# Graph layer on one core: the output projection of one node block per turn of the edge loop instead of a stage of its own

## The reference

```python
h = jnp.maximum(_layernorm(x, axis=-1), 0.0)
eq = h @ Wq + bq
ek = h @ Wk + bk
e = efeat @ We + be
m = jax.nn.relu(eq[dst] + ek[src] + e)
ft = jax.ops.segment_sum(m, dst, num_segments=n_nodes)
return x + (ft @ Wr + br)
```

## Time and profile before

| | us |
| --- | --- |
| median of 3 runs | 1247.06 (1246.17 to 1247.19) |
| the profiled execution | 1248.51 |
| its span | 1246.6 |
| TensorE matmul busy | 1119.9 (90%) |
| VectorE busy | 962.8 (77%) |
| ScalarE busy | 857.2 (69%) |
| GpSimd busy | 887.7 (71%) |

### The profile page before, as it was taken

How to read it: one execution, slowest core, us unless ns; L and a number is a source line. 1 busy time by engine, 2 the same in 40 slices (tenths; PEclk the granted TensorE clock), 3 DMA queues, 4 the chain that set the end, 5 groups by cost and what they waited for, 6 DMA issues and landing times.

```text
span 1246.6 us, 33342 instructions
## 1 busy us (share of the span) xinstructions
PE 1119.9 (90%) x8632; PEld 1051.0 (84%) x8632; DVE 962.8 (77%) x1324; ACT 857.2 (69%) x1463; POOL 887.7 (71%) x946
## 2 busy tenths in 40 slices
PE   1997799999999999999999999999999999999876
PEld 1775789889898888898898988888988989898875
DVE  5887577777777777777777777777777777777798
ACT  1676577777777777777777777777777777777542
POOL 4454777777777777777777777777777777777644
PEclk9999999999999999999999999999999999999989
DMA  8888777777778777777777777777877787877664
GB/s 249 273 275 273 237 244 246 245 244 243 254 246 248 245 246 247 250 248 244 244 245 251 244 252 245 244 247 247 251 246 245 245 248 242 256 244 244 209 191 140
DMA packets 164469, 303.48 MB, mean 243 GB/s; under 512 B 29204, under 2 KB 110740, under 8 KB 164452
## 3 DMA queue, kind: packets, MB, share of 16 engines
q1 hardware_dynamic: 124516, 194.18, 50.0%
q0 software_dynamic: 39936, 109.11, 27.0%
HBM read 275.69 MB, written 27.48 MB: 243 GB/s over the span
## 4 chain that ended last, share of the span: by engine, by line
POOL 46%; issue 37%; PE 9%; DVE 3%; DMA 3%; ACT 1%; POOLq 1%; SPq 0%; DVEq 0%; ACTq 0%
POOL k_rows L494 46%; PE p_sum L934 5%; PE p_edge L934 3%; DVE hT_lo L896 1%; DMA ft<-in_x 1%; PE p_turn L943 1%; DMA k_rows<-k_table,idx 1%; POOLq L502 0%; DMA pre<-in_dst_groups 0%; DMA range_table<-top_g 0%; DVE k_rows L908 0%; DVE k_rows L717 0%; POOLq L492 0%; DVE p_edge L838 0%; ACT hT_hi L655 0%
## 5 line engine op out<-in xcount | busy, mean ns | idle before, releaser
L494 POOL DMA_INDIRECT k_rows<-k_table,idx x832 | 799.3, 961 | 255.9 <-issue 255.0
L934 PE MATMUL p_edge<-we_hi,edge_hi 128*128 128x256 f32 x1664 | 487.0, 293 | 75.9 <-DVE m_lo L846 67.1
L934 PE MATMUL p_edge<-we_lo,edge_hi 128*128 128x256 f32 x1664 | 465.4, 280 | 0.0
L934 PE MATMUL p_edge<-we_hi,edge_lo 128*128 128x256 f32 x1664 | 465.1, 280 | 0.0
L838 DVE TENSOR_TENSOR p_edge<-p_edge,k_rows 128x1024 f32<-128x1024 f32 x208 | 256.4, 1233 | 244.7 <-DMA k_rows<-k_table,idx 244.6
L934 PEld LDWEIGHTS p_edge<-we_hi,edge_hi 128*128 128x128 f32 x1664 | 314.4, 189 | 122.2 <-issue 66.9
L615 ACT ACTIVATE m_hi<-p_edge 128x1024 fp32r<-128x1024 f32 x208 | 213.8, 1028 | 262.2 <-DVE p_edge L838 262.2
L934 PEld LDWEIGHTS p_edge<-we_lo,edge_hi 128*128 128x128 f32 x1664 | 315.1, 189 | 0.0
L934 PEld LDWEIGHTS p_edge<-we_hi,edge_lo 128*128 128x128 f32 x1664 | 313.2, 188 | 0.0
L818 DVE TENSOR_TENSOR edge_lo<-edge,edge_hi 128x1024 fp32r<-128x1024 f32 x208 | 253.6, 1220 | 0.9 <-ACT edge_hi L594 0.9
L846 DVE SCALAR_TENSOR_TENSOR m_lo<-p_edge,m_hi 128x1024 fp32r<-128x1024 f32 x208 | 253.2, 1217 | 1.3 <-ACT m_hi L615 1.3
(11 more groups left out here) (81 smaller groups left out, 937.8 us busy)
## 6 DMA issues: line engine op xcount, KB each, us to landing
edge<-in_edges SPq DMA_DIRECT2D x208, 512.0 KB, 4.0
rel_row<-rel_table SPq DMA_DIRECT2D x208, 96.0 KB
q_win<-q_table SPq DMA_DIRECT2D x416, 48.0 KB
q_table<-m_hi SPq DMA_DIRECT2D x52, 256.0 KB, 2.6
k_rows<-k_table,idx POOLq DMA_INDIRECT x832
ft<-in_x SPq DMA_DIRECT2D x4, 1664.0 KB, 12.7
k_table<-k_rows SPq DMA_DIRECT2D x52, 128.0 KB, 2.9
out_rows<-k_rows SPq DMA_DIRECT2D x13, 512.0 KB, 3.1
```

What stands on the lines that cost most here:

```text
L494: nc.gpsimd.indirect_dma_start(out=k_rows[:, slot, j, :], out_offset=None, in_=k_table, in_offset=bass.IndirectOffsetOnAxis(ap=idx[:, slot ...
L934: ins = nc.tensor.matmul(target, a(h), b[:, h, :], start=(h == 0 and n == 0), stop=(stop and h == HALVES - 1 and n == 2))
```

## The change

The output projection moves into the main loop. In turn t the block t-6 is projected (in the first six turns blocks 46 to 51 in its place, whose result is overwritten or padding), and blocks 46 to 48 are left for the end (TAIL). The parts of a turn are: ScalarE ft_high at the end of its first step, VectorE ft_low in its second step between edge_low and message_low and finish at the end of its fourth, TensorE emit at the end of its third, SyncE one store and one load of 128 rows of x in its third. Two adds into ft get one more wait each, since they mustn't write a block that is being read. br is no longer added by GpSimd but by two matmuls of one row (a row of ones with br's high and low part) at the start of each product. GpSimd has no output work. The test for a single pass also looks whether the destinations are far enough along (in_order), by four more small instructions; br is split by one on ScalarE and one on VectorE; two constants are made at the start. Three loads of x for the tail are issued ahead of the loop. Line numbers of the changed kernel differ from those of before.

```diff
-X_SLOTS = 8
-OUT_SLOTS = 4
 LOAD_TURNS = SIDE_TURNS + UNROLL
 LEAD = 2
-assert TURNS % OUT_SLOTS == 1 and OUT_SLOTS == TILES and UNROLL == OUT_SLOTS and X_SLOTS == UNROLL + 4
+OUT_LAG = 6
+OUT_BODIES = BODIES - OUT_LAG
+TAIL = tuple(range(OUT_BODIES, -(-NODES // LANES)))
+OUT_SPAN = (OUT_LAG - 2) * LANES
+assert BLOCKS == BODIES and (PASSES - 1) * WIN >= OUT_BODIES * LANES and len(TAIL) < NRING
...
+        behind = sb("behind", [LANES, 1], F32)
+        in_order = sb("in_order", [LANES, 1], F32)
...
-        bias_r = sb("bias_r", [LANES, D], F32)
+        br_hi = sb("br_hi", [1, D], F32R)
+        br_lo = sb("br_lo", [1, D], F32R)
+        ones = sb("ones", [1, LANES], F32R)
...
+        out_x = pre[:, 0].rearrange("p (s d) -> p s d", d=D)
+        result = pre[:, 1].rearrange("p (s d) -> p s d", d=D)
...
+        br_raw = sum_rows[0:1, 0, :]
+        body_base, ahead = win_f, spans
+        gap = rel_g[0:2 * WIN, 0, :]
...
+        p_res = p_turn[:, 1, 0:D]
...
+        SPAN_STEPS = 4 + 7
+        PREP_STEPS = SPAN_STEPS + 4 + CHUNKS + 2
+        def out_block(it):
+            return (it + OUT_BODIES) % BODIES
...
+            for t, b in enumerate(TAIL):
+                sp.dma_start(out_x[:, 1 + t, :], x_blocks[b]).then_inc(s_xtail, 16)
+            def load_out_x(it):
+                source = one_block(x_blocks, out_block(it))
+                after(sp, s_fin, it - 1)
+                sp.dma_start(out_x[:, 0, :], source).then_inc(s_xo, 16)
+            def store_out(it):
+                target = one_block(out_blocks, out_block(it))
+                after(sp, s_fin, it)
+                sp.dma_start(target, result[:, 0, :]).then_inc(s_out, 16)
+            def loads(it, first=False):
                 for u in range(UNROLL):
                     load_edge(it, u)
                     load_row(it, u)
                     load_window(it, u)
-            def load_xo(t):
-                x_turn = x_blocks[NRING * t:NRING * (t + 1)].rearrange("b p d -> p b d")
-                sp.dma_start(x_slots[t % X_SLOTS], x_turn)\
-                    .then_inc(s_xo[t % X_SLOTS], 16)
-            for t in range(UNROLL):
-                sp.wait_ge(s_ehi, bodies * UNROLL - (UNROLL - 1) + t)
-                sp.wait_ge(s_elo, bodies * UNROLL - (UNROLL - 1) + t)
-                load_xo(t)
-            sp.wait_ge(s_send, bodies * UNROLL)
-            for t in range(UNROLL, X_SLOTS - 1):
-                load_xo(t)
-            sp.wait_ge(s_mhi, bodies * UNROLL - 1)
-            sp.wait_ge(s_mlo, bodies * UNROLL - 1)
-            load_xo(X_SLOTS - 1)
-            for t in range(TURNS):
-                after(sp, s_fin, PAIRS * (t + 1) - 1)
-                sp.dma_start(out_blocks[NRING * t:NRING * (t + 1)].rearrange("b p d -> p b d"),
-                             result[:, t % OUT_SLOTS]).then_inc(s_out[t % 2], 16)
-                if t + X_SLOTS < TURNS:
-                    after(sp, s_xbr, t)
-                    load_xo(t + X_SLOTS)
-                if t > 0:
-                    sp.wait_ge(s_out[(t - 1) % 2], 16 * ((t - 1) // 2 + 1))
-                    sp.sem_inc(s_free, 1)
-            sp.wait_ge(s_out[(TURNS - 1) % 2], 16 * ((TURNS - 1) // 2 + 1))
+                    if u == 2:
+                        if not first:
+                            store_out(it - 2)
+                        load_out_x(it - 1)
+            loads(1, first=True)
+            with sp.Fori(2, bodies) as it:
+                loads(it)
+            store_out(bodies - 2)
+            load_out_x(bodies - 1)
+            store_out(bodies - 1)
+            sp.wait_ge(s_out, bodies * 16)
+            sp.sem_inc(s_go_sp, 1)
+            for t, b in enumerate(TAIL):
+                sp.wait_ge(s_fin, bodies + t + 1)
+                sp.dma_start(out_blocks[b], result[:, 1 + t, :]).then_inc(s_tail, 16)
+            sp.wait_ge(s_tail, 16 * len(TAIL))
...
-            pool.wait_ge(s_pre, bodies * UNROLL)
-            for t in range(TURNS):
-                pool.wait_ge(s_xo[t % X_SLOTS], 16 * (t // X_SLOTS + 1))
-                after(pool, s_free, t - OUT_SLOTS)
-                nc.gpsimd.tensor_tensor(result[:, t % OUT_SLOTS], x_slots[t % X_SLOTS],
-                                        bias_r[:].unsqueeze(1).to_broadcast([LANES, NRING, D]),
-                                        ALU.add).then_inc(s_xbr, 1)
...
+                    nc.scalar.activation(br_hi[:], br_raw, ACT.Copy).then_inc(s_esplit, 1)
...
+            def ft_high(it):
+                block_cols = bass.ds(out_block(it) * LANES, LANES)
+                after(act, s_ft, it * UNROLL - 3)
+                after(act, s_outp, it - 1)
+                act.sem_inc(s_go_act, 1)
+                nc.scalar.activation(hT_hi[:, 0, :].rearrange("p (h n) -> p h n", h=HALVES),
+                                     ft[:, :, block_cols], ACT.Copy).then_inc(s_fhi, 1)
...
+                    if u == 0:
+                        ft_high(it)
...
+                link(nc.vector.scalar_tensor_tensor(ahead[:], ranges[:, 0, :], float(NODES - WIN), body_base[:],
+                                                    ALU.min, ALU.subtract))
+                link(nc.vector.tensor_reduce(behind[:], ahead[:], axis=AX.X, op=ALU.min))
+                link(nc.vector.tensor_scalar(in_order[:], behind[:], float(-OUT_SPAN), None, ALU.is_ge))
                 link(nc.vector.tensor_scalar(narrow[:], span[:], float(WIN - 1), None, ALU.is_le))
+                link(nc.vector.tensor_tensor(narrow[:], narrow[:], in_order[:], ALU.mult))
...
+                nc.vector.tensor_tensor(br_lo[:], br_raw, br_hi[:].bitcast(F32), ALU.subtract)\
+                    .then_inc(s_esplit, 1)
...
-            def add_sum(it, u, w0):
...
+            def add_sum(it, u, w0, read=None, split=None):
                 _, slot, n, _, _ = visit(it, u)
                 after(dve, s_turn, n)
+                if read is not None:
+                    after(dve, s_fhi, read)
+                if split is not None:
+                    after(dve, s_flo, split)
                 after(dve, s_ft, n - 1)
                 window = ft[:, :, bass.ds(w0, WIN)]
                 turned = p_turn[:, 0, 0:D].rearrange("p (h n) -> p h n", h=HALVES)[:, :, 0:WIN]
                 nc.vector.tensor_tensor(window, window, turned, ALU.add).then_inc(s_ft, 1)
+            def ft_low(it):
+                block_cols = bass.ds(out_block(it) * LANES, LANES)
+                after(dve, s_ft, it * UNROLL - 2)
+                after(dve, s_fhi, it)
+                after(dve, s_outp, it - 1)
+                nc.vector.tensor_tensor(hT_lo[:, 0, :].rearrange("p (h n) -> p h n", h=HALVES),
+                                        ft[:, :, block_cols],
+                                        hT_hi[:, 0, :].bitcast(F32).rearrange("p (h n) -> p h n", h=HALVES),
+                                        ALU.subtract).then_inc(s_flo, 1)
+            def finish(it):
+                after(dve, s_outp, it)
+                dve.wait_ge(s_xo, (it + 1) * 16)
+                if not (isinstance(it, int) and it == 0):
+                    dve.wait_ge(s_out, it * 16)
+                nc.vector.tensor_tensor(result[:, 0, :], p_res, out_x[:, 0, :], ALU.add).then_inc(s_fin, 1)
             def steps(it, first=False, last=False):
                 for u in range(UNROLL):
@@ -868,10 +907,14 @@
                     add_rows(it, u, last)
                     make_send(it, u)
                     if not (first and u < 3):
-                        add_sum(it, u - 3, w0)
+                        add_sum(it, u - 3, w0, read=it if u == 1 else None, split=it if u == 2 else None)
                     if not (last and u + 2 >= UNROLL):
                         edge_low(it, u + 2)
+                    if u == 1:
+                        ft_low(it)
                     message_low(it, u)
+                    if u == 3:
+                        finish(it)
...
+            def out_product(target, u):
+                for n, b in enumerate((br_hi, br_lo)):
+                    nc.tensor.matmul(target, ones[:], b[:], start=(n == 0), stop=False)
+                return split_product(target, lambda h: hT_hi[:, u, h * LANES:(h + 1) * LANES],
+                                     lambda h: hT_lo[:, u, h * LANES:(h + 1) * LANES], wr_hi, wr_lo, start=False)
+            def emit(it):
+                after(pe, s_fhi, it)
+                after(pe, s_flo, it)
+                after(pe, s_fin, it - 1)
+                out_product(p_res, 0).then_inc(s_outp, 1)
             def steps(it, first=False, last=False):
                 for u in range(UNROLL):
                     if not (last and u + 1 >= UNROLL):
@@ -1022,10 +1056,12 @@
                         window_sum(it, u - 1)
                     if not (first and u < 2):
                         turn_part(it, u - 2)
+                    if u == 2:
+                        emit(it)
...
+            for t in range(len(TAIL)):
+                pe.wait_ge(s_flo, bodies + t + 1)
```

(1 more changed line is left out.)

114 lines of the change are left out of this document (36 added, 78 removed).

## The result

The changed kernel takes 1203.19 us (median of 4 runs, 1201.38 to 1204.34), the kernel before 1246.62 (1245.06 to 1247.19): 0.9652 of it, with an interval of 0.9635 to 0.9669. The prediction was 1208, with a range of 1195 to 1226. The profiled execution took 1204.34, its span 1202.5, so the span is 44.1 shorter than before. Of the eleven executions of experiment 5 nine took 1232 to 1240 us and two 1250 and 1252, and the profiled one is of these two.

The account below looks back on a forecast made before the run. GpSimd's gathers were taken to pace the loop. Span: 1246.6 - 62.1 (old output stage) + 10.8 (new end) + 11.2 (ft_low in loop) + 1.1 (before loop) = 1207.6 us, so 1208 for the median; range 1195 to 1226.

Parts of the forecast that it names:

- Gathers pace the loop: Main loop: GpSimd never waits for data; a gather costs 1.25 us, a turn of 16 some 20.1 us.
- ft_low delays the third by 0.22: Turn's second step: the third gather starts inside ft_low and ends at 607.69 instead of 607.47, in turns 1 to 51.
- The first rival: VectorE, second step: ft_low costs the loop nothing, so 1197 us (1194 to 1200); chance 0.17.
- The loop term, +11.2: Main loop: ft_low's 0.22 us on the pacing engine in each of turns 1 to 51 adds 11.2 us.
- TensorE has the room: TensorE after the third step: emit's 0.94 us per turn fits into waits of 1.2 per turn; cost 0.
- third rival, 1216: TensorE becomes the bound through slower one-row matmuls: 0.16 per turn missing, 8 us, 1216; chance 0.05.
- finish costs 0: VectorE, last step: finish's 0.4 us and three waits fit in 1.29 us of idle time; cost 0.
- second rival, slower: Turn's first add slides and edge_lo delays the third gather, up to 1258; chance 0.10 faster, 0.01 unchanged, 0.05 slower.
- ScalarE and SyncE cost 0: In the loop: ScalarE's 0.4 us ft_high and SyncE's 128 KB load and store per turn are absorbed; cost 0 each.
- Front, +1.1: Before the loop: four small VectorE instructions and br_hi, br_lo add 1.1 us; bounds 0.3 and 2.
- New end, 10.8: After the loop: finish ahead of the last adds, ft_low, 24 matmuls, finish and last store, summing to 10.8 us.

Follow-up runs that it names:

- experiment 5: Changed kernel with TensorE computing the block's product twice in each turn of the loop; 1234.5 us, 0.9916 of the kernel before.
- experiment 1: Changed kernel with ft_low behind m_lo instead of ahead of it in the turn's second step; 1196.1 us, 0.9589 of the kernel before.
- experiment 2: Changed kernel with finish of the turn before and then ft_low behind m_lo in the second step; 1191.4 us, 0.9552 of the kernel before.
- experiment 3: Changed kernel with ft_low reading p_res in PSUM instead of hT_hi in SBUF; 1190.4 us, 0.9551 of the kernel before.
- experiment 9: Kernel before plus one unused VectorE instruction of ft_low's form between edge_lo and m_lo, with slower transfers; 1616.9 us, 1.0017 of the kernel before.
- experiment 12: Changed kernel with finish's addition done six times, a repeated run with slower transfers; 1597.2 us, 0.988 of the kernel before.
- experiment 4: Changed kernel without the two one-row br matmuls in the loop's product; 1201.8 us, 0.9637 of the kernel before.
- experiment 6: Changed kernel with finish's addition done four times; 1204.3 us, 0.9658 of the kernel before.
- experiment 7: Changed kernel with ft_low done twice, the first into an unused place; 1200.5 us, 0.9633 of the kernel before.

## Why the prediction was right, step by step

- **Gathers pace the loop, and ft_low delays the third by 0.22.** Shown: 1.473 - 1.257 = 0.216 per turn, 11.0 us in 51; experiments 1 to 3 move it and take it away. The first rival, ft_low free of charge (1197), falls, but it was close: the lead of 0.08 us was 0.07 in fact, and a gather within 0.015 would have gone free (experiment 9).
- **The loop term, +11.2, measured +7.5.** What was mis-sized is not ft_low but the rest: the ordinary distance between gathers fell from 1.2575 to 1.2535, 3.3 us over 832. That I had held fixed. In the nine traces with the change's code in which the gathers pace it is 1.2535 or 1.250, and in experiment 9, made from the kernel before, the gathers with no two-input VectorE instruction beside them took 0.956 us against 0.945 in experiment 12, where transfers were slow as well. So it seems to come with the program, as far as two traces of the old form tell, and the cause stays open. This is where most of the 5 us between 1208 and 1203 went, and nothing in the prediction earned them.
- **TensorE has the room (third rival, 1216).** Right: waits for m_lo fell to 16.2 (predicted some 20), experiment 4 gains nothing but noise. Its term was too small: a one-row matmul and the first matmul behind it stand 0.20 to 0.23 apart instead of 0.12, so from the product's first matmul to the next group's first it is 1.24 us, not 0.94 but the rival's 1.26; the rival erred in that TensorE didn't run out. Of 20.35 us it has 0.6 left. Experiment 5 shows that the next 1.25 don't fit, and that in its profiled execution the bill is written by edge_lo over a gather and not by TensorE.
- **finish costs 0 (second rival, slower).** Right with more room than I gave it: three more of 0.34 cost nothing (experiment 6). The rival itself, a late first add, was never brought about where it could be timed; what its collision costs was seen in experiment 5, through another cause: 0.94 per turn.
- **ScalarE and SyncE cost 0.** Nothing in the gathers' distances is left for them.
- **Front, +1.1, measured +0.1.** One profile of each doesn't settle it: the first gather comes between 120.95 and 121.79 in the changed kernels but for one at 123.80, at 121.42 and 119.13 in the two of the old form. br_lo alone took 0.95 us instead of the 0.3 assumed. The term is uncertain by 2 us or more.
- **New end, 10.8.** Of it 0.3 were for finish ahead of the last add, where nothing was seen (from the last gather to that add's end 11.4 us after 11.5), and 10.5 for the rest, measured 10.5. The sum is right, its parts aren't. The products were put at 5.5: 24 times 0.214, from 14 matmuls in 3.00 us at a granted clock of 0.50, and 0.35 for the first of them and the drain. That the clock would be 0.50 in the new end too, and the 0.35, were my estimates, which no trace showed. The products took 7.0 us (1192.96 to 1199.97), since at this clock the one-row matmuls and their neighbours stand 0.34 to 0.38 apart and not 0.214; from the end of the last finish to the end it is 2.1 and not 3.5. That the two cancel is luck. So in part is the granted clock: it was 0.50 as forecast in this execution, but in those of experiments 1, 5 and 7 it was 1.00 and the same products took 2.9 us less.

## What to carry to other kernels

Look for the engine that never waits for data, however short its busy time, and not for the one that the chain names: here that was GpSimd at 72% busy, with TensorE at 94% and 58% of the chain beside it. When an instruction with two SBUF inputs is put on VectorE beside a paced stream of gathers, look whether a gather starts inside it: here one did in each turn and took 1.17 us instead of 0.95, and moved behind an instruction that reads PSUM, ft_low left it at 0.95 at the same length of 0.42 (experiment 2). After such a change look at each position of the turn by itself: one distance of 1.47 among fifteen of 1.25 to 1.30 names the instruction at fault. And before two executions are compared to 3 us, look at the granted clock of their ends.
